# A slot-pipelined mixture-of-experts layer: where the expert selection, the second state x2, the normalised row xn and one gate product stand in each engine's order

## The reference

```python
x = x.reshape(B, -1, 256, D)[:, :, ::2, :]            # every second row: tiles of 128 rows
h = softmax(x x^T / sqrt(D)) x                        # attention inside a tile
xn = layernorm(h)
h2 = h + xn + gate * corr(decay_matrix @ conv(xn, bind), unbind)   # a decaying sum over the rows of a sequence
xf = layernorm(h2)
logits = gelu(xf @ router_w1 + b) @ router_w2 + b     # 8 experts, the best two are taken
idx, w = top_k(softmax(logits), 2)
v, integrated = 0, xf
for _ in range(2):                                    # two iterations
    ctx = concat(integrated, v)
    a, b, g = gelu(ctx @ w1 + b1) @ w2 + b2           # for the shared branch and for both experts
    v_next = sigmoid(a) * v - softplus(b) * (x - mu)
    x_next = x + 0.1 * sigmoid(g) * v_next
    halt = sigmoid(gelu(integrated @ halt_w1) @ halt_w2)
    integrated += halt * (weighted sum of the branches' x_next - integrated); v likewise
out = h2 + xf + integration_weight * (gelu(integrated @ refine_w1) @ refine_w2)
```

## Time and profile before

| | us |
|---|---|
| median of 3 runs (lowest, highest) | 841.17 (841.04, 843.41) |
| the profiled execution | 841.62 |
| its span, first to last instruction | 839.8 |

### The profile page before, as it was taken

How to read it: one execution, slowest core, us unless ns; L and a number is a source line. 1 busy time by engine, 2 the same in 40 slices (tenths; PEclk the granted TensorE clock), 3 DMA queues, 4 the chain that set the end, 5 groups by cost and what they waited for, 6 DMA issues and landing times.

```text
span 839.8 us, 14631 instructions
## 1 busy us (share of the span) xinstructions
PE 763.6 (91%) x4784; PEld 656.4 (78%) x4784; DVE 657.5 (78%) x1516; ACT 534.9 (64%) x1334; POOL 291.7 (35%) x393
## 2 busy tenths in 40 slices
PE   4578999999999999999999999999999999999885
PEld 3466788888888888888888888888888888888764
DVE  3456778888888888888888889889889889889643
ACT  1555567667666666676676676675675675675444
POOL 1134333343343353253343343334334334334121
PEclk9577999999999999999999999999999999999997
DMA  9000000000000000000000000000000000000000
GB/s 342 33 7 1 1 1 14 1 14 13 1 13 13 2 14 13 2 13 7 7 14 2 14 14 1 13 14 1 14 13 2 7 8 1 7 7 1 7 7 12
DMA packets 8154, 14.13 MB, mean 17 GB/s; under 512 B 848, under 2 KB 7048, under 8 KB 7568
## 3 DMA queue, kind: packets, MB, share of 16 engines
q1 hardware_dynamic: 8080, 13.20, 4.5%
HBM read 10.05 MB, written 3.15 MB: 16 GB/s over the span
## 4 chain that ended last, share of the span: by engine, by line
DVE 47%; PE 19%; ACT 19%; issue 11%; POOL 2%; DVEq 1%; DMA 1%; ACTq 0%; SPq 0%; POOLq 0%
PE ctl L448 6%; DVE work L1070 6%; DVE hm_hi L1040 4%; DVE work L1220 4%; DVE both L1175 4%; ACT L776 3%; ACT ge L809 3%; DVE both L1177 3%; PE cd L611 3%; PE pa L425 3%; ACT L787 3%; DVE work L1215 3%; DVE t L1180 2%; ACT work L779 2%; DVE vu L1225 2%
## 5 line engine op out<-in xcount | busy, mean ns | idle before, releaser
L347 POOL TENSOR_TENSOR hm_lo<-gl,mexp 128x256 fp32r<-128x256 f32 x144 | 111.3, 798 | 345.5 <-DVE gl L1054 345.5
L448 PE MATMUL ctl<-w2e_hi,hm_hi 128*128 128x512 f32 (+1 forms) x432 | 161.8, 384 | 12.4 <-DVE hm_hi L1040 9.6
L448 PE MATMUL ctl<-w2e_lo,hm_hi 128*128 128x512 f32 (+1 forms) x432 | 149.8, 361 | 0.0
L827 ACT ACTIVATE work<-ctl 128x256 f32<-128x256 f32 (+1 forms) x144 | 70.6, 490 | 103.8 <-PE ctl L467 103.8
L448 PEld LDWEIGHTS ctl<-w2e_hi,hm_hi 128*128 128x128 f32 x432 | 82.3, 191 | 35.2 <-DVE hm_hi L1040 23.7
L464 PE MATMUL ctl<-w2e_hi,hm_lo 128*128 128x512 f32 (+1 forms) x432 | 101.1, 360 | 0.0
L1040 DVE TENSOR_TENSOR hm_hi<-ge,mexp 128x256 fp32r<-128x256 f32 x144 | 79.4, 578 | 21.8 <-ACT ge L809 15.3
L448 PEld LDWEIGHTS ctl<-w2e_lo,hm_hi 128*128 128x128 f32 x432 | 82.7, 192 | 11.2
L425 PE MATMUL pa<-x1T,par 128*128 128x128 f32 x768 | 89.7, 275 | 0.0
L425 PEld LDWEIGHTS pa<-x1T,par 128*128 128x128 f32 x768 | 87.8, 192 | 0.1
L464 PEld LDWEIGHTS ctl<-w2e_hi,hm_lo 128*128 128x128 f32 x432 | 75.3, 190 | 14.8 <-POOL hm_lo L347 0.8
(11 more groups left out here) (167 smaller groups left out, 1738.5 us busy)
## 6 DMA issues: line engine op xcount, KB each, us to landing
work<-params_dram SPq DMA_DIRECT2D x3, 1152.0 KB, 9.8
out_dram<-y SPq DMA_DIRECT2D x24, 128.0 KB, 1.7
xa<-x_dram SPq DMA_DIRECT2D x16, 128.0 KB, 3.0
par<-params_dram SPq DMA_DIRECT2D x1, 1280.0 KB, 12.4
work<-params_dram SPq DMA_DIRECT2D x2, 512.0 KB, 10.8
xa<-x_dram SPq DMA_DIRECT2D x8, 119.0 KB
par<-params_dram SPq DMA_DIRECT2D x1, 512.0 KB, 15.5
par<-params_dram SPq DMA_DIRECT2D x1, 465.0 KB, 4.2
```

Of the source, the lines that this page charges most:

```text
L347: TT(hm[1][:, j, c, :], gl[:, c, :], pairs(tile, j, c), ALU.mult).then_inc(done, 1)
L448: mm(dst[:, a:z], hm[0][:, j, c, :], w2e[i][:, c, a:z], start=(c == 0 and i == 0), stop=False)
L827: AF(tan[tile.s][:, 1:kinds, j, :], ctl_t[:, D:kinds * D].rearrange("p (a d) -> p a d", a=kinds - 1), ACT.Tanh, scale=0.5)
```

## The change

Six edits, which belong together in pairs:

1. DVE: the selection of tile f and `shared_lo` come before the x2 block of tile m. They used to come after it.
2. PE: the masks are turned right after `expert_hi` of branch 1, ahead of the second half of tile f's hidden layer. x2 is turned after that half and after `expert_end`, ahead of `expert_lo`. It waits for ACT's copy of the turned masks, since both use the same PSUM bank. The masks' spreading in the next slot waits for x2T as well.
3. ACT: the turned masks are copied before the gelus of tile f, and x2T is copied after them.
4. DVE: the last step of the gates becomes `velocity_gates` and runs after the scans.
5. PE: xn is turned after the second expert branch of tile t.
6. POOL: rg_lo comes before hx.

```diff
@@ POOL
                     TT(rs1[:, :], vpe1[:, :], mhalf_t[:, :], ALU.pow).then_inc(rs1_g, 1)
-                    passed(pool, xn_v, f)
-                    passed(pool, mv2_v, f, back=1)
-                    TT(hx[:, :], h[:, :], xn[:, :], ALU.add).then_inc(hx_g, 1)
                 if o.exists():
                     passed(pool, rgh_sb, o)
                     passed(pool, rl2_ps, o, back=1)
                     TT(rgp[1][:, :, :], rg[:, :, :], rgp[0][:, :, :].bitcast(fp32), ALU.subtract).then_inc(rgl_g, 1)
+                if f.exists():
+                    passed(pool, xn_v, f)
+                    passed(pool, mv2_v, f, back=1)
+                    TT(hx[:, :], h[:, :], xn[:, :], ALU.add).then_inc(hx_g, 1)
@@ PE
                     passed(pe, mT_sb, t)
+                    if o.exists():
+                        passed(pe, x2T_sb, o)
                     both = maskT[:, :, :].rearrange("e j m -> e (j m)")
...
+                if t.exists():
+                    expert_end(ctl[0], 1, t, en1_v, 2 * D)
+                    expert_lo(ctl[0], 1, t, hl1_g, eb1_sb, u1_ps, 2 * D)
+
                 if f.exists():
                     passed(pe, xn_v, f)
...
                     last.then_inc(xnT_ps, 1)
-
-                if t.exists():
-                    expert_end(ctl[0], 1, t, en1_v, 2 * D)
-                    expert_lo(ctl[0], 1, t, hl1_g, eb1_sb, u1_ps, 2 * D)
...
                         expert_hi(ctl[1], 1, n, hm2_v, a, b)
+                if f.exists():
+                    if f.low == 0:
+                        pe.wait_ge(set_act, 2)
+                    passed(pe, mask_v, f)
+                    passed(pe, xfT_sb, f)
+                    for j in range(2):
+                        last = mm(pc[0:MR, j * P:(j + 1) * P], mask[:, j, 0:MR], identb[:, :], start=True, stop=True)
+                    last.then_inc(mT_ps, 1)
+                    hidden(pa, P, w1e, range(EC // 2, EC), xfT, KD, e1_ps)
+
+                if n.exists():
+                    expert_end(ctl[1], 1, n, en2_v, 3 * D)
                 if m.exists():
                     passed(pe, x2_v, m)
                     if f.exists():
-                        passed(pe, xfT_sb, f)
+                        passed(pe, mT_sb, f)
...
                     last.then_inc(x2T_ps, 1)
-                if f.exists():
-                    hidden(pa, P, w1e, range(EC // 2, EC), xfT, KD, e1_ps)
-                    (wait for mask_v, the masks turned, mT_ps: as above)
-                if n.exists():
-                    expert_end(ctl[1], 1, n, en2_v, 3 * D)
+                if n.exists():
                     expert_lo(ctl[1], 1, n, hl2_g, eb2_sb, u2_ps, 3 * D)
@@ ACT
-                if m.exists():
-                    state(x2T, D, m, x2T_ps, x2T_sb, rl1_ps)
-
                 if f.exists():
+                    passed(act, mT_ps, f)
+                    passed(act, u2_ps, f, back=NS, per=BR)
+                    AF(end[f.s][0:MR, :, :], ...)
+                    AF(maskT[:, :, :].rearrange("p j m -> p (j m)"), pc[0:E, 0:2 * P], ACT.Copy).then_inc(mT_sb, 1)
...
                     expert_units(f, e1_ps, e1_sb)
-                    passed(act, mT_ps, f)
-                    (the two copies, as above)
+                if m.exists():
+                    state(x2T, D, m, x2T_ps, x2T_sb, rl1_ps)
@@ DVE
                 link(last)
+            def velocity_gates(m):
                 V.scalar_tensor_tensor(tan[m.s][:, 0, :, :], tan[m.s][:, 2, :, :], 1.0, gw[:, :, :], ALU.add, ALU.mult)
...
                     last.then_inc(scan_v, 1)
+                if m.exists() and not last_in:
+                    velocity_gates(m)
...
                 if f.exists():
                     (selection and shared_lo, now here)
+                if m.exists():
+                    if last_in:
+                        gates(m)
+                        velocity_gates(m)
+                        products(m)
+                    (the x2 block, which stood ahead of the selection)
```

More of the change, by code:

```diff
@@ L721, in slot @@
                     last.then_inc(x2T_ps, 1)
-                if f.exists():
-                    hidden(pa, P, w1e, range(EC // 2, EC), xfT, KD, e1_ps)
-                    if f.low == 0:
-                        pe.wait_ge(set_act, 2)
-                    passed(pe, mask_v, f)
-                    if m.exists():
[L730 to L735, removed]
                 if n.exists():
-                    expert_end(ctl[1], 1, n, en2_v, 3 * D)
                     expert_lo(ctl[1], 1, n, hl2_g, eb2_sb, u2_ps, 3 * D)
@@ L944, in slot @@
                     unit(n, 1, u2_sb, u2_ps, ctl[0], 3)
-                if m.exists():
-                    state(x2T, D, m, x2T_ps, x2T_sb, rl1_ps)
                 if f.exists():
+                    passed(act, mT_ps, f)
+                    passed(act, u2_ps, f, back=NS, per=BR)
+                    AF(end[f.s][0:MR, :, :], pc[0:MR, 0:2 * P].rearrange("p (j m) -> p j m", j=2), ACT.Copy)
+                    AF(maskT[:, :, :].rearrange("p j m -> p (j m)"), pc[0:E, 0:2 * P], ACT.Copy).then_inc(mT_sb, 1)
                     if n.exists():
@@ L956, in slot @@
                     expert_units(f, e1_ps, e1_sb)
-                    passed(act, mT_ps, f)
-                    passed(act, u2_ps, f, back=NS, per=BR)
-                    AF(end[f.s][0:MR, :, :], pc[0:MR, 0:2 * P].rearrange("p (j m) -> p j m", j=2), ACT.Copy)
-                    AF(maskT[:, :, :].rearrange("p j m -> p (j m)"), pc[0:E, 0:2 * P], ACT.Copy).then_inc(mT_sb, 1)
+                if m.exists():
+                    state(x2T, D, m, x2T_ps, x2T_sb, rl1_ps)
                 if n.exists():
@@ L1169, in slot @@
                     end_lo(n, 1, gl2_v, hm2_v, en2_v)
[L1171 to L1185, removed]
                 if f.exists():
@@ L1211, in slot @@
                     shared_lo(f, s1_sb, sh1, sab1, sl1_v)
+                if m.exists():
[3 more added lines that the diff above has]
+                        products(m)
+                    link(V.tensor_tensor(both[:, :, :], both[:, :, :], tan[m.s][:, 0:2, 2, :], ALU.add))
+                    passed(dve, u1_g, m)
+                    link(V.tensor_tensor(both[:, :, :], both[:, :, :], vu[m.s][:, :, :], ALU.mult))
+                    passed(dve, th2_sb, m)
+                    V.tensor_scalar(h2c[:, :], th2[:, m.s:m.s + 1], 0.025, 0.025, ALU.mult, ALU.add)
+                    link(V.scalar_tensor_tensor(t1[:, :], both[:, 0, :], 0.5, both[:, 1, :], ALU.mult, ALU.subtract))
+                    passed(dve, x2T_ps, m, back=1)
+                    V.scalar_tensor_tensor(x2[:, :], t1[:, :], h2c[:, :], x1[m.s][:, :], ALU.mult,
+                                           ALU.add).then_inc(x2_v, 1)
+                if o.exists() and not n.exists():
+                    output(o)
                 if t.exists():
```

## The result

| | before | after |
|---|---|---|
| median us (lowest, highest) | 841.11 (840.65, 843.41) | 813.84 (811.85, 817.57) |
| the profiled execution's span | 839.8 | 812.6 |
| slot 3 to 20, mean | 32.01 | 30.88 |
| masks to second masks, slot 12 | 17.32 | 16.37 |
| second masks to the next masks, slot 12 | 14.73 | 14.53 |

The ratio of the times is 0.9676 [0.9636, 0.9715]: 3.2% faster. The two half slots of the table are read between the rows of `gl` (L1054), one in each set of masks.

A forecast was written before the change was run, and what follows sets the result against it. The bound was taken to be a loop mostly through DVE, crossing to PE and ACT at L611. 18 x (0.83 + 0.08) = 16.4 plus 1.6, 0.4, 0.2, 0.7 took 19.3 from 841.6: 822 us, range 818 to 827, wider 815 to 833.

The forecast's parts named there:

- The loop and its two measures: Whole slot: masks to L611 10.28 us, L611 to second masks 7.00, then the next slot; earlier L611 and next masks count.
- Edits 4 to 6: First half of a slot: gates' product behind the scans, third L1070 0.55 later, L611 0.83 us earlier.
- The 0.1 that I gave h2: First half, DVE after L611: h2 row late by about 0.1 us behind L1072, covered by 0.6 of wait.
- Edits 1 to 3: Second half: POOL's delay moves from x2 block to selection, 4.04 + 2.4 = 6.4 against 6.49 us, a gain of 0.08.
- slot 1's row: Second half: slot 1 has no x2 block, so its selection follows the masks directly; its 4.04 us was taken for every slot.
- Stop at x2: End of slot, PE at L720: waits 0.5 us for x2, the loss covered by the 0.34 wait at the next masks.
- The working's 418.95: PE's arrival at the next masks after the x2 stop: 418.95 instead of 418.92; uncovered the loss would be 0.3.
- The sum: Whole run: 16.4 for slots 3 to 20, then 1.6, 0.4, 0.2 and 0.7, together 19.3 us off 841.6.
- The drain's term: End of the run: `expert_end` (0.90 us) runs in the 1.86 for which PE waits for x2, worth 0.7.
- Gain halved: Rival, first half: port turns between DVE and POOL cost more, 0.45 us a slot, 832 us; chance 0.2.
- POOL holds both blocks: Rival, second half: x2 block keeps 3.76 behind a selection of 4.04, slot 0.4 us longer, 851 us; chance 0.08.
- The turns come out well: Rival, whole slot: selection not held, block free, PE the bound, 1.35 us a slot, 814 us; chance 0.12.

The follow-up runs named there:

- b4: Edits 4 and 5 alone (gate product behind the scans, xn turned behind the second branch) on the kernel before: 817.48 us, ratio 0.9716.
- a1: Edits 4, 5 and 6 alone on the kernel before, the end of the slot as before: 821.36 us, ratio 0.9771.
- c2: Kernel after without edit 6, POOL's two base rows of tile t swapped with u of tile m: 804.92 us, ratio 0.9548 to the kernel before.
- b1: Edit 4 alone (gate product behind the scans) on the kernel before: 826.79 us, ratio 0.9822.
- a2: Edits 1, 2 and 3 alone on the kernel before; gates, xn and POOL as before: 834.94 us, ratio 0.9932.
- c1: Kernel after with all six edits, POOL's two base rows swapped with u of tile m: 807.12 us, ratio 0.9594 to the kernel before.
- b3: Edit 1 alone (selection ahead of x2 on DVE, PE's and ACT's orders as before) on the kernel before: 856.85 us, ratio 1.0181.

## Where the prediction was right and where it missed

**The loop and its two measures.** Right. The slot is set by masks to L611 to second masks to next masks. After L611 it takes 7.00 again (415.31 to 422.31), as forecast.

**Edits 4 to 6.** The mechanism is right in each row that was named: xn's row near 1.4 (1.31), L1075 at 0.96 (0.93), L1128 about 8.5 after the slot's start (8.43). The term was mis-sized: L611 comes 0.94 earlier, forecast 0.83. The third L1070 ends at +8.40, 0.34 later than before and not 0.55: xn's row ended 0.14 behind rg_lo where I gave it 0.25, hx and u kept their forecast lengths from there (hx ended at +7.50 for a forecast of +7.65), and the third L1070 ended 0.15 behind u, not 0.20. The 0.1 that I gave h2 didn't come: it still starts 1.17 after the product (416.48 - 415.31), and the half is shorter by 0.95, as L611 is earlier. What I did not see is that edit 6 is a loss for its own sake. I put its price into the sum (0.55 of the 1.32), but never asked what the change would be without it. The runs price it at 0.21 at L611 (9.13 in b4, 9.34 after and in a1) and 0.3 for the half.

**Edits 1 to 3.** The sign of each part is right: the delay moved from one block to the other. The size is small and was taken too small: 0.20 against 0.08, and by its own terms it was smaller still, 6.49 - (4.04 + 2.4) = 0.05. The selection is 3.92 where slot 1's row gave 4.04, the block 2.38 where I took 2.4. In c2 POOL has one row there in place of two, and the selection's loss against the 2.73 of before falls from 1.19 to 0.72: POOL's rows beside it are the cause, one turn each: `count` is free again and `tied` isn't.

**PE's stops.** Stop at x2 about 0.5: 0.3 for the matmuls, 0.6 for the weight loads ahead of them. None at the masks and none at the next L448: both right. (The working's 418.95 for PE's arrival at the next masks doesn't follow from its terms, which give 418.92 - 0.34 + 0.27 = 418.85; the conclusion stands.) The waits of the weight loads from 380 to 700 us, before and then after:

```profile
PEld ctl L448 <- DVE hm_hi L1040: 9.1, 20, 0.6
...
PEld cd L734 <- DVE mask L1202: 2.5, 10, 0.3
```
```profile
PEld cd L736 <- DVE x L1215: 6.3, 10, 0.8
PEld ctl L450 <- DVE hm_hi L1040: 5.6, 10, 0.6
```

Twenty waits for masks have become ten, those of the second masks, where ACT's row comes last; L734's are gone.

**The sum.** Forecast 19.3, measured 27.2 on the profiled executions. The step that failed is the size of the terms, in two groups. Slots 3 to 20 gave 1.13 each in place of 0.91, 3.9 us in all: 0.11 at L611 and 0.12 in the second half. That alone makes 822.3 into 818.4, which would still have been inside the range. The other 4.0 lie at the ends: 1.7 in the start and 2.3 in the drain. The drain's term was `expert_end` inside a wait, 0.7. What the drain gained goes mostly with TensorE's clock. The windows of the last stretch, where a1's order of the drain is the old one and so is b1's (same columns as the earlier trace rows); before, after, a1, b1:

```profile
789.80:799.80 10.00, 7.12 (x46) 6.56 (x45) 3.10 (x6) 3.23 (x9) 0.00 (x0) 0.83 0.01 2
809.80:819.80 10.00, 7.00 (x31) 5.63 (x32) 5.18 (x11) 3.22 (x8) 0.00 (x0) 0.83 0.01 2
```
```profile
762.60:772.60 10.00, 6.99 (x50) 6.05 (x49) 5.96 (x12) 3.06 (x8) 0.00 (x0) 1.00 0.00 0
782.60:792.60 10.00, 6.24 (x38) 4.96 (x37) 6.91 (x15) 5.01 (x11) 0.28 (x1) 1.00 0.01 2
```
```profile
769.20:779.20 10.00, 7.12 (x52) 6.12 (x51) 5.70 (x12) 2.79 (x7) 0.00 (x0) 1.00 0.01 2
789.20:799.20 10.00, 5.89 (x35) 4.92 (x36) 6.56 (x15) 4.66 (x11) 0.01 (x1) 1.00 0.01 2
```
```profile
775.10:785.10 10.00, 7.39 (x49) 7.15 (x50) 2.05 (x5) 3.73 (x10) 0.24 (x1) 0.83 0.01 2
795.10:805.10 10.00, 7.14 (x37) 5.95 (x36) 5.05 (x11) 3.51 (x7) 0.00 (x0) 0.83 0.01 2
```

From slot 23 to the end: before 69.95 and b1 71.05, both with two stretches at 0.83 (a part of each at 1.2 GHz); a1 67.22 and after 66.95, both at 2.4 GHz there. a1 and b1 don't hold edits 1 to 3, and edits 5 and 6, in which they differ, do nothing once tile f is gone, that is from slot 23 on: the same order of work takes 3.8 us more in one than in the other. So 2.7 of the drain's 3.0 came without the term that I named; between a1 and after, at the same clock in these windows, edits 1 to 3 leave 0.3 for it.

Why the clock falls in one kernel's drain and not in another's isn't settled: after shows the short drain in both profiled executions (66.95, 67.03), and in the edits I see no reason. The clock also differs between executions of one kernel: the kernel after took 811.85 us at a mean granted clock of 0.975 and 817.57 at 0.962, the kernel before, on a1's chip, 837.98 at 0.973 and 841.94 at 0.962. The start moves too, with no edit that I can put it to: 131.91 in a1 and 131.63 in a2, which together are the change and neither of which gains there, 130.44 in b1, 129.09 in c2 and 125.66 in c1. So the cause of the 4.0 us at the ends stays open: the drain's part went along with the clock, and for the start's part no run shows a cause. I left this out of the range, and it was the range's error: an end of some 70 us at a clock that can go either way is worth 2 to 4 us by itself.

**The rivals.** "Gain halved" and "POOL holds both blocks" fell: the block is free after the selection (0.69). "The turns come out well", 814, has the time that was measured but not its reason: it asked for a free selection and PE as the bound, and the selection is 3.92. PE as the bound is nearer to c2's state. The halved gain would have been a slot 0.45 shorter; it is 1.13 shorter.

## What to carry to other kernels

When an edit is one of several, price it alone, in both directions: here one of six costs time everywhere (edit 6), one loses 1.8% unless another comes with it (edits 1 and 2), and one is what keeps another's delay from reaching PE (5 and 6). Before reordering rows of an engine, look what POOL runs beside each place: what decides is how many POOL rows stand in line there, and having one beside the selection in place of two was worth another 8 us (815.30 to 807.12). And give the start and the drain, where TensorE's clock isn't full throughout, a term for it in the range.

## What the runs showed of the hardware

DVE rows of 8 columns are held by POOL's rows like those of 256 or 512: `tied` (tensor_scalar, 128x8) 0.78 and the scan `count` (128x8) 0.65 beside POOL rows of 0.73, against 0.23 and 0.17 when none runs. In these two cases the row lasts as long as POOL's: they end at 396.76 and 397.56, POOL's at 396.73 and 397.53. And `tied` starts 0.02 ahead of the POOL row that holds it (395.98, 396.00), so the order of two starts in a trace doesn't tell which of them has to wait.

One stop of 1.8 us in PE's row (b3) was followed by a window at a granted clock of 0.83 in the middle of the run, where the kernels before and after show 1.00; behind the nine like it from 380 to 700 us the clock stayed at 1.00.
